# A three-layer interaction network on one core: exact and GpSimd products in one ring of ten, neighbouring couples multiplied by one instruction

## What is computed

```python
x0 = inputs                      # (512, 39, 16)
xk = inputs
for idx, (W, b) in enumerate(params):          # W: (39, fields of xk, 128)
    z = jnp.einsum('bhd,bkd,hks->bsd', x0, xk, W) + b[None, :, None]
    z = jax.nn.relu(z)
    if idx != n_layers - 1:
        half = z.shape[1] // 2                 # 64
        xk = z[:, :half, :]
        direct.append(z[:, half:, :])
    else:
        direct.append(z)
logit = jnp.sum(jnp.concatenate(direct, axis=1), axis=-1)      # (512, 256)
```

## Time and profile before

| | us |
|---|---|
| median of 3 runs (562.15 to 562.33) | 562.28 |
| the profiled execution's own time | 562.33 |
| its span in the profile | 560.5 |
| PE matmuls busy | 551.9 (98%) |
| DVE busy | 535.9 (96%) |
| POOL busy | 499.5 (89%) |
| ACT busy | 379.4 (68%) |
| DMA, mean over the span | 218 GB/s |

### The profile page before, as it was taken

The page is one execution under the profiler, slowest core; times in us unless marked ns, Lnnn a source line. Parts: engine busy times, 40 slices in busy tenths (PEclk is TensorE's granted clock), DMA queues, the critical chain, the costliest instruction groups (busy, mean ns, idle before and its releaser), DMA issues.

```text
span 560.5 us, 6190 instructions
## 1 busy us (share of the span) xinstructions
PE 551.9 (98%) x2008; PEld 374.9 (67%) x2008; DVE 535.9 (96%) x496; ACT 379.4 (68%) x427; POOL 499.5 (89%) x228
## 2 busy tenths in 40 slices
PE   7999999999999999999999999999999999999997
PEld 2435667667677677777767677677777767677665
DVE  4679999999999999999999999999999999999985
ACT  0436577776858767676776858777676876858662
POOL 0438899899999989999899999989999899999986
PEclk9999999999999999999999999999999999999999
DMA  8997391844828266391845828276391845826200
GB/s 326 418 408 317 132 370 34 325 191 181 344 87 331 108 254 271 146 361 30 331 183 183 342 95 333 98 262 263 150 363 29 333 177 192 333 99 215 81 1 20
DMA packets 21056, 122.17 MB, mean 218 GB/s; under 512 B 2720, under 2 KB 2976, under 8 KB 10784
## 3 DMA queue, kind: packets, MB, share of 16 engines
q1 hardware_dynamic: 20736, 121.51, 56.0%
q10 hardware_dynamic: 288, 0.26, 0.2%
HBM read 121.24 MB, written 0.52 MB: 217 GB/s over the span
## 4 chain that ended last, share of the span: by engine, by line
PE 82%; DVE 10%; issue 3%; ACT 2%; DMA 1%; POOL 1%; SPq 0%; DVEq 0%; POOLq 0%; ACTq 0%
PE z L611 82%; DVE raw L426 4%; DVE exact L426 3%; DVE d_raw L426 2%; DMA fields<-x_fields 1%; DVE lo L440 1%; POOL lo L515 1%; ACT hi L656 1%; ACT maps L675 0%; ACT final L696 0%; ACT L675 0%; DVE sums L453 0%; DVE sums L447 0%; SPq L358 0%; SPq L337 0%
## 5 line engine op out<-in xcount | busy, mean ns | idle before, releaser
L515 POOL TENSOR_TENSOR lo<-raw,hi 128x1024 fp32r<-128x1024 f32 x198 | 469.1, 2410 | 12.1 <-ACT hi L656 11.6
L656 ACT ACTIVATE hi<-raw 128x1024 fp32r<-128x1024 f32 (+1 forms) x213 | 219.1, 1029 | 125.1 <-DVE raw L426 112.0
L611 PE MATMUL z<-hi,w_hi 128*128 128x512 f32 (+1 forms) x559 | 220.8, 399 | 0.9 <-ACT hi L656 0.4
L426 DVE TENSOR_TENSOR raw<-spread,maps 128x1024 f32<-128x1024 f32 x184 | 219.0, 1210 | 2.1 <-ACT maps L675 2.1
L611 PE MATMUL z<-hi,w_lo 128*128 128x512 f32 x513 | 202.5, 395 | 0.0
L611 PE MATMUL z<-lo,w_hi 128*128 128x512 f32 x544 | 196.7, 451 | 0.2 <-POOL lo L515 0.2
L611 PE MATMUL z<-exact,w_exact 128*128 128x512 f32 (+1 forms) x386 | 180.4, 594 | 2.8 <-DVE exact L426 2.0
L611 PEld LDWEIGHTS z<-lo,w_hi 128*128 128x128 f32 x544 | 101.2, 188 | 56.2 <-issue 31.5
L611 PEld LDWEIGHTS z<-hi,w_hi 128*128 128x128 f32 (+1 forms) x559 | 104.8, 188 | 31.4 <-ACT final L696 3.7
L611 PEld LDWEIGHTS z<-exact,w_exact 128*128 128x128 f32 (+1 forms) x386 | 72.1, 189 | 68.0 <-issue 53.7
L611 PEld LDWEIGHTS z<-hi,w_lo 128*128 128x128 f32 x513 | 96.2, 188 | 22.9 <-issue 0.5
(11 more groups left out here) (21 smaller groups left out, 69.6 us busy)
## 6 DMA issues: line engine op xcount, KB each, us to landing
spread<-x_spread SPq DMA_DIRECT2D x80, 1024.0 KB, 8.1
fields<-x_fields SPq DMA_DIRECT2D x31, 768.0 KB, 6.8
fields<-x_fields SPq DMA_DIRECT2D x15, 512.0 KB, 5.6
w_exact<-w SPq DMA_DIRECT2D x10, 256.0 KB, 14.7
spread<-x_fields SPq DMA_DIRECT2D x1, 768.0 KB, 10.1
raw<-w SPq DMA_DIRECT2D x1, 640.0 KB, 6.7
spread<-x_fields SPq DMA_DIRECT2D x1, 512.0 KB, 10.7
out<-sums SPq DMA_DIRECT2D x2, 240.0 KB, 4.2
```

Source lines behind the costliest of these rows:

```text
L426: nc.vector.tensor_tensor(products, by_field, by[0:rows, :].unsqueeze(1).to_broadcast([rows, tiles, COLS]), ALU.mult).then_inc(ready, 1)
L515: nc.gpsimd.tensor_tensor(low_part(layer, c, k), raw[low_rows(layer, k), PLACE[S][layer, c, k] % RAW_RING, 0:tiles_in(layer, k), :], hi[lo ...
L611: mm = nc.tensor.matmul(z_of(layer, c)[:, :], w[0:rows, :], part[0:rows, :], start=(step == FIRST_STEP[layer, c] and p == 0), stop=(step = ...
L656: nc.scalar.activation(hi[0:rows, count % HI_RING, 0:tiles, :], products, ACT.Copy).then_inc(hi_ready, 1)
```

## The change

1. The rings `exact` (4) and `raw` (6) become one ring `raw` of 10 couples, which E and S couples take in the order of the program. The two semaphores for finished products become one, `products_ready`. A place is free when what held it ten E or S couples ago is done: the exact matmuls of an E couple, the POOL subtraction of an S couple.
2. Couples k and k+1 (k even) of layers 1 and 2, neither of kind D, are multiplied by one DVE instruction of 2,048 columns, where both lie in the same segment and side by side in the ring (not over its end), from chunk 1 on. It counts `products_ready` up by two when it ends.
3. `sums` shrinks to 8 chunks in use at a time; SP stores every four chunks, 64 KB a half, eight DMAs in all.
4. The staged weights of layer 0 lie in a slot of `spread` in place of the `raw` ring.

Kinds and order are as they were: `KINDS_ODD` and `KINDS_LAST` hold the same strings as `KINDS`.

```diff
-EXACT_RING = 4
-RAW_RING = 6
+RAW_RING = 10
+
+MERGED = ("M", "MMMMM", "MMMMM")
...
+        def raw_place(layer, c, k):
+            return PLACE["ES"][layer, c, k] % RAW_RING
+
+        def wait_products_free(engine, count):
+
+            if count >= RAW_RING:
+                couple = COUPLE["ES"][count - RAW_RING]
+                if couple in PLACE[E]:
+                    engine.wait_ge(exact_used, PLACE[E][couple] + 1)
+                else:
+                    engine.wait_ge(s_lo_ready, S_LOW[couple] + 1)
+
+        def merged(layer, c, k, couples):
+
+            return (k % 2 == 0 and k + 1 in couples and k // 2 < len(MERGED[layer]) and MERGED[layer][k // 2] == "M"
+                    and D not in kinds(layer, c)[k:k + 2] and raw_place(layer, c, k) + 1 < RAW_RING
+                    and (layer > 0 and c > 0 or c > 1))
...
             def multiply(layer, c, couples):
+                both = 0
                 for k in couples:
+                    if both:
+                        both = 0
+                        split_lo_after(layer, c, k, couples)
+                        continue
                     kind = kinds(layer, c)[k]
-                    count = PLACE[kind][layer, c, k]
                     tiles = tiles_in(layer, k)
+                    if merged(layer, c, k, couples):
+                        both, tiles = 1, 4
...
-                    if kind == E:
-                        if count >= EXACT_RING:
-                            dve.wait_ge(exact_used, count - EXACT_RING + 1)
-                        products, ready = exact[0:rows, count % EXACT_RING, 0:tiles, :], exact_ready
-                    elif kind == S:
-                        if count >= RAW_RING:
-                            dve.wait_ge(s_lo_ready, S_LOW[COUPLE[S][count - RAW_RING]] + 1)
-                        products, ready = raw[0:rows, count % RAW_RING, 0:tiles, :], raw_ready
...
+                    else:
+                        place = raw_place(layer, c, k)
+                        for couple in range(k, k + both + 1):
+                            wait_products_free(dve, PLACE["ES"][layer, c, couple])
+                        products = raw[:, place:place + both + 1, :, :].rearrange("p r t c -> p (r t) c")[0:rows, 0:tiles, :]
+                        ready = products_ready
                     nc.vector.tensor_tensor(products, by_field,
                                             by[0:rows, :].unsqueeze(1).to_broadcast([rows, tiles, COLS]),
-                                            ALU.mult).then_inc(ready, 1)
+                                            ALU.mult).then_inc(ready, 1 + both)
```

More of the change, by code:

```diff
@@ L317, in low_part, with columns, wait_stored @@
             return lo[:, USED[layer, c, k] % LO_RING, :, :]
+        def columns(c):
+            a = c % (2 * STORED) * EXAMPLES
+            return slice(a, a + EXAMPLES)
+        def wait_stored(engine, half, c):
+            if c >= 2 * STORED and c % STORED == 0:
+                engine.wait_ge(stored[half], 16 * (c // STORED - 1))
         def z_of(layer, c):
@@ L355, in load_weights, with store @@
                 sp.dma_start(w_exact[n][:, a:e, :], (None, w1, w2)[n][:, a:e, :]).then_inc(w_loaded[n][p], 16)
+            def store(half, part):
+                a = part * STORED * EXAMPLES
+                sp.wait_ge((direct_summed, last_summed)[half], (part + 1) * STORED)
+                sp.dma_start(out[half * OUT:(half + 1) * OUT, a:a + STORED * EXAMPLES],
+                             sums[:, half, columns(part * STORED).start:columns(part * STORED).start
+                                  + STORED * EXAMPLES]).then_inc(stored[half], 16)
             load_fields(0, 0)
@@ L378, in _ @@
                     load_spread(c + 1, q)
[L380 to L389, removed]
+                if c > STORED and c % STORED == 1:
+                    for half in range(2):
+                        store(half, c // STORED - 1)
+            for half in range(2):
+                store(half, CHUNKS // STORED - 1)
+            for half in range(2):
+                sp.wait_ge(stored[half], 16 * CHUNKS // STORED)
         @block.vector
@@ L402, in multiply @@
                             dve.wait_ge(early_loaded[k], 16)
-                        elif k < 3:
-                            dve.wait_ge(fields_loaded[k], (c if c and k == 1 else c + 1) * 16)
+                        else:
+                            for p in range(k, min(k + both, 2) + 1):
+                                dve.wait_ge(fields_loaded[p], (c if c and p == 1 else c + 1) * 16)
                         by = early[:, 0, :] if ahead else copies if c else field_copies
@@ L433, in multiply, with split_lo_after @@
                         split_lo(layer, c, k)
+            def split_lo_after(layer, c, k, couples):
+                if k - D_LAG in couples and kinds(layer, c)[k - D_LAG] == D:
+                    split_lo(layer, c, k - D_LAG)
             def split_lo(layer, c, k):
@@ L652, in split_hi @@
                     wait_high_free(act, count)
-                    place = PLACE[kind][layer, c, k]
                     rows, tiles = ROWS_REST if rest(layer, k) else 128, tiles_in(layer, k)
-                    products = raw[0:rows, place % RAW_RING, 0:tiles, :] if kind == S else d_raw[0:rows, 0:tiles, :]
+                    products = raw[0:rows, raw_place(layer, c, k), 0:tiles, :] if kind == S else d_raw[0:rows, 0:tiles, :]
                     nc.scalar.activation(hi[0:rows, count % HI_RING, 0:tiles, :], products,
```

52 lines of the change are left out of this document (30 added, 22 removed).

## The result

The changed kernel takes **564.45 us** (median of 6 runs, 564.26 to 564.57), the kernel before 562.24 (6 runs). The ratio is 1.0038, 95% interval 1.0028 to 1.0049: slower by 0.38%. I had forecast 563.3 us and a range up to 564.4; the end of the range was missed by 0.05. The profiled execution took 564.45 us, 2.12 more than the profiled one before (562.33); its span is longer by 2.12 too (562.66 against 560.54, shown rounded on the pages). In some executions of most of these kernels TensorE's granted clock was lower behind the start-up's first matmuls, and everything after them is 0.85 us later; neither of these two is such.

What follows compares the result with a forecast made beforehand. PE's matmuls were taken as the bound, with DVE hardly behind. -0.10 up to chunk 14 (0.37 + 0.19 - 0.66), +1.00 for the tail and +0.1 for the store gave +1.0 us, 563.3 us; range 561.6 to 564.4.

Steps and rivals of the forecast that it cites:

- The bound: Steady part: PE's matmuls bound, DVE barely keeps pace; a faster DVE gives back only 0.06 us a chunk.
- The merged instruction: DVE, 2,048 columns: about 2.28 us, 81 of them, each saving about 0.065 us of DVE.
- Step 1: Layer-2 head of chunk 1, pair unmerged: DVE, `final` and the waiting PE come 0.19 us earlier.
- Step 2: Layer-2 head of chunk 2, merged: 0.89 later less 0.52 gained, so PE starts 0.37 us later.
- Step 3: End of layer 1 in chunk 2's period: POOL is 1.07 late, PE's wait grows, +0.19 us once.
- Step 4: Steady chunks: the loop over maps1 takes 33.08 against PE's 33.52; 0.06 gained in 11 periods, -0.66 us.
- the wait for maps1: Sign in steady chunks: DVE stands about a third of a microsecond a chunk for maps1, which costs nothing.
- Step 6: Layer 2 of the last chunk: POOL's row of five lo moves by 1.07 without cover, PE +1.00 us.
- Step 7: End of the program: the last store is 64 KB, not 16, +0.1 us, at most 0.56.
- The slower rival: Merged instruction longer than its columns say; at 2.45 us DVE bounds every chunk, 568.5 us; chance 0.06.
- The tail hides it: Last chunk: POOL's row catches up, 562.3 us, or 561.6 if earlier delays are hidden too; chance 0.10.

Runs made afterwards that it cites:

- the shorter sums: Kernel before, with both DVE sums over d taken over 4 of the 16 numbers: 560.96 us, ratio 0.9970.
- the kernel without heads: The change, but couples (2, c, 0-1) stay two instructions in every chunk: 562.25 us, ratio 0.9999.
- the kernel without chunk 1: The change with merging only from chunk 2 on: 564.45 us.
- the ring alone: The change with `MERGED` empty: ring of ten, moved staging and four-chunk stores, no merged instruction: 562.61 us, ratio 1.0008.
- the trace with the small store: The change with the last store of each half cut in two, so that the final piece is 16 KB: 564.49 us.
- the run with one merged instruction: The change with only (2, 15, 0-1), in the last chunk, merged: 563.71 us.
- the kernel without heads from chunk 2: The change with couples (2, c, 0-1) left as two and nothing merged in chunk 1: 562.06 us, ratio 0.9994.
- the merged heads of twelve chunks: The change with only couples (2, c, 0-1) of chunks 2 to 14 merged (chunk 11's pair lies over the ring's end): 563.62 us.

## Why the prediction was right where it was, and where not

I had given slower a chance of 0.43 and no difference 0.47; the measured 0.38% is clearly the first. The direction of the forecast was right; its size, +1.0 us, is half of what was measured, 2.2 between the medians and 2.12 between the profiled executions. By its steps:

- **The bound.** Right in what hangs on it: with DVE relieved, matmuls fill the period, a weight load's wait of about 0.12 is no loss, and 0.05 to 0.06 a chunk is all there is (shown by the shorter sums, and by the kernel without heads: 33.53, where 33.52 was predicted). Its wording was too strong: before the change the engine that set the 33.58 was DVE, since taking 0.47 us a chunk from PE changed nothing. By what the Trainium skill says of the busy share of weight loads (Perfetto Trace Analysis, Identifying the Most-Contended Engine) PE would still have room in the period with shorter sums, its loads being 23.88 of 33.60 us; no room was there.
- **The merged instruction.** 2.277 us and 81 of them, as worked out.
- **Step 1, chunk 1: -0.19.** Measured +0.35 (0.17 of it before the head). The split of the last weights on ACT stands behind the hi of (1, 1, 8), which is late too; I had looked for such a place at the heads of layer 2 only. It cost nothing in the end.
- **Step 2, chunk 2: +0.37.** +0.90, with the 0.35 above. `final` is late by the 0.88 that was estimated; what was missing is DVE's gain of 0.52: DVE starts the head at 105.03, and 105.01 before, since the gain was lost in chunk 1. Without merging in chunk 1 three merged instructions are ahead of this head, 0.89 less 3 x 0.065 is 0.70, and 0.65 was measured.
- **Step 3, POOL, +0.19 once.** Right at first (0.90 to 1.09), wrong in "once".
- **Step 4, -0.66: the step that failed.** PE gains its 0.05 at the heads, but at the end of layer 1 of about every other chunk it stops again behind POOL, for 0.02 to 0.1. From chunk 3 to the last it gained 0.29 (1.09 to 0.80), and in the kernel without chunk 1 0.05 (0.81 to 0.76). The sum knew one loop, from PE's head over maps1 to `final`, and worked it out at 33.08 with 0.44 to spare. It left out the one that closed: from PE over the rings to DVE's head, then hi, eleven lo on POOL and PE again at the end of layer 1, a wait that step 3 took as paid once. DVE could not run far enough ahead to end it: its stretch in the loop over maps1 is 23.38 (249.42 to 272.80), not 23.09, with waits at the rings of hi and lo in it. That the rings bound DVE's lead is read from the waits; a larger ring was not tried. Of the wait for maps1 of a third of a microsecond a chunk, which was to show DVE's lead, there is next to none; DVE waits at its lo instead, 0.12 to 0.19 a chunk.
- **Step 6, the tail, +1.00.** 1.13 on PE, 1.10 by the run that does this alone.
- **Step 7, the store, +0.1.** 0.19 in the traces of the change and of the ring alone, of which 0.14 go with the 64 KB by the trace with the small store.

Together: 0.17 + 0.18 + 0.55 + 0.19 for steps 1 to 3 where 0.37 plus 0.19 were given (+0.53), -0.29 for -0.66 (+0.37), 1.13 for 1.00 (+0.13) and 0.19 for 0.1 (+0.09); that is the 1.1 us between 1.0 and the 2.12 of the profiled executions. The whole error is on one side, because each place that I had not looked at could only hold something back.

The slower rival, an instruction longer than its columns, is out by the 2.277. "The tail hides it" is out by the run with one merged instruction.

## What to carry to other kernels

Before joining two instructions, list for every joined pair who is standing idle for its first half; a pair inside a queue cost nothing here, a pair behind a handover made everything downstream late by its whole first half (in the steady part once, and not again at each head), and one such pair in the last, uncovered stage cost more than 68 other pairs gained. A faster engine helps by no more than the gaps of the next engine in line, and those have to be read from starts; and where several loops come within a percent of the period, moving work earlier on one makes a full loop through another longer: look at which rings the new lead runs into.

## What was unexpected in the hardware and the program

- A lag can be set by a loop and not by what first caused it: PE was 0.80 or 0.76 us behind at the end of layer 1 of the last chunk, whether it had been 1.09 or 0.81 behind in chunk 3.
- Three limits within 1% of one period: PE 33.53, DVE 33.58, and POOL's row through `final` 33.80 once the first hi is 1.1 us later. Taking 0.47 us a chunk from PE alone gave nothing (562.40 against 562.39), 0.8 from DVE gave 0.05 a chunk.
- In some executions the granted clock was lower behind the start-up's first matmuls. Below the same stretches of the kernel without heads from chunk 2, where PE had been busy 4.64 of the 8 us before, and of the change, with 5.45 of 8 (stretch, PE, PEld, DVE, ACT, POOL busy, then clock, DMA, GB/s):

```profile
0.00:8.00 8.00, 4.64 (x6) 1.74 (x6) 2.07 (x4) 0.00 (x0) 0.20 (x4) 1.00 0.74 259
8.00:10.00 2.00, 1.97 (x3) 0.97 (x4) 1.52 (x2) 0.00 (x0) 0.00 (x0) 0.63 1.03 430
10.00:14.00 4.00, 4.00 (x8) 1.58 (x7) 3.31 (x4) 0.00 (x0) 0.00 (x0) 0.76 1.02 420
```

```profile
0.00:8.00 8.00, 5.45 (x7) 1.92 (x7) 2.10 (x4) 0.00 (x0) 0.20 (x4) 1.00 0.75 260
8.00:10.00 2.00, 1.93 (x4) 0.62 (x4) 1.52 (x2) 0.00 (x0) 0.00 (x0) 1.00 1.03 427
10.00:14.00 4.00, 3.48 (x8) 1.35 (x8) 3.30 (x4) 0.00 (x0) 0.00 (x0) 1.00 1.02 418
```

A mean of 0.63 and 0.76 is a mixture of the lower level, 1.2 GHz, and the full 2.4; it costs 0.85 us, nearly as much as the merged heads of twelve chunks (1.01). The difference in PE's busy time before it is no difference in work: the same six start-up matmuls run in both, the last of them 0.48 us behind the fifth in the first trace and 0.85 in the second. Before two single profiles are compared here, their starts have to be.
